# Block 1 of a four-block kernel: the queries and keys of the second sequence are projected in the four steps ahead of the first exponentials

## What is computed

```
qkv = (x @ Wqkv).reshape(Bx, Nx, 3, H, HD).transpose(2, 0, 3, 1, 4)
q, k, v = (qkv[0], qkv[1], qkv[2])
attn = jnp.einsum('bhnd,bhmd->bhnm', q, k) * (SCALE / TEMPERATURE)
attn = attn * alpha[None, :, None, None] + beta[None, :, None, None]
attn = jax.nn.softmax(attn, axis=-1) * gamma[None, :, None, None]
...
enhanced_v = v * (1.0 + ka)
out = jnp.einsum('bhnm,bhmd->bhnd', attn, enhanced_v)
```

## Time and profile before

| | |
|---|---|
| median of 3 runs | 2335.92 us (2332.85 to 2339.22) |
| the profiled execution | 2333.25 us, of which the span from first to last instruction is 2331.4 |
| PE busy | 2239.6 us, 96% of the span |
| DVE, ACT, POOL busy | 1635.1 (70%), 1254.6 (54%), 732.4 (31%) us |
| chain that ended last | PE 73%, DVE 14%, DMA 4%, ACT 4% |
| mean granted TensorE clock | 0.989 |

### The profile page before, as it was taken

The page is one execution under the profiler, slowest core; times in us unless marked ns, Lnnn a source line. Parts: engine busy times, 40 slices in busy tenths (PEclk is TensorE's granted clock), DMA queues, the critical chain, the costliest instruction groups (busy, mean ns, idle before and its releaser), DMA issues.

```text
span 2331.4 us, 42446 instructions
## 1 busy us (share of the span) xinstructions
PE 2239.6 (96%) x16257; PEld 1316.2 (56%) x16306; DVE 1635.1 (70%) x4252; ACT 1254.6 (54%) x2823; POOL 732.4 (31%) x730
## 2 busy tenths in 40 slices
PE   7999999999998999989899999999999999999998
PEld 3333333334634867756566666666666666666665
DVE  6788888886502746668777677677767777787763
ACT  4666666665222622247666656665665665566640
POOL 3344323321111411144433233333333333333321
PEclk7999999999998999999999999999999999999999
DMA  7454343333397020010000000000001000000001
GB/s 240 151 158 121 117 119 122 112 91 109 157 422 297 2 91 19 28 39 3 5 6 6 5 2 6 6 2 32 15 6 53 6 15 24 19 6 24 22 23 40
DMA packets 68617, 158.44 MB, mean 68 GB/s; under 512 B 6256, under 2 KB 49120, under 8 KB 63936
## 3 DMA queue, kind: packets, MB, share of 16 engines
q1 hardware_dynamic: 65856, 146.55, 17.8%
q0 software_dynamic: 2560, 9.18, 1.7%
HBM read 116.39 MB, written 35.13 MB: 65 GB/s over the span
## 4 chain that ended last, share of the span: by engine, by line
PE 73%; DVE 14%; DMA 4%; ACT 4%; issue 3%; POOL 1%; SPq 0%; another core or an unknown queue 0%; POOLq 0%; DVEq 0%; ACTq 0%
PE banks L2073 10%; PE banks L2051 7%; PE banks L1932 6%; PE banks L1946 5%; PE banks L232 4%; PE banks L274 4%; PE banks L2033 3%; PE banks L245 3%; PE banks L1976 3%; PE banks L1991 3%; DMA arena<-in_e_W 3%; DVE arena L483 2%; PE banks L1455 2%; PE banks L1958 2%; PE banks L300 2%
## 5 line engine op out<-in xcount | busy, mean ns | idle before, releaser
L483 DVE TENSOR_REDUCE arena<-banks 128x1 f32<-128x512 f32 x512 | 322.6, 681 | 61.2 <-PE banks L232 60.4
L395 ACT ACTIVATE arena<-banks 128x512 f32<-128x512 f32 x512 | 280.3, 596 | 136.1 <-PE banks L245 112.4
L2073 PE MATMUL banks<-arena 128*128 128x512 f32 x640 | 293.2, 594 | 1.0 <-DVE arena L2258 1.0
L2155 ACT ACTIVATE arena<-arena 128x256 f32<-128x256 f32 (+1 forms) x512 | 286.5, 562 | 5.0 <-DVE arena L2264 4.5
L2411 POOL TENSOR_TENSOR arena<-arena 128x512 f32<-128x512 f32 x128 | 162.8, 1272 | 379.8 <-DVE arena L2295 379.8
L1932 PE MATMUL banks<-arena 128*128 128x512 f32 x512 | 241.5, 594 | 2.8 <-DVE arena L2295 2.8
L232 PE MATMUL banks<-arena 96*128 96x512 bf16 x512 | 202.9, 400 | 14.6 <-DVE arena L483 8.9
L2407 POOL TENSOR_TENSOR arena<-arena 128x16 f32<-128x16 f32 x64 | 189.4, 2959 | 5.4
L2127 ACT ACTIVATE arena<-arena 128x256 f32<-128x256 f32 (+1 forms) x256 | 102.1, 471 | 162.9 <-DVE arena L2240 162.9
L2073 PEld LDWEIGHTS banks<-arena 128*128 128x128 f32 x640 | 115.5, 190 | 126.7 <-issue 116.5
L245 PE MATMUL banks<-arena 128*128 128x512 bf16 x463 | 174.6, 382 | 3.1 <-ACT arena L395 2.2
(11 more groups left out here) (304 smaller groups left out, 4225.7 us busy)
## 6 DMA issues: line engine op xcount, KB each, us to landing
arena<-in_e_W SPq DMA_DIRECT2D x16, 2048.0 KB, 15.6
arena<-stacks SPq DMA_DIRECT2D x64, 384.0 KB, 4.7
arena<-in_e_Wg SPq DMA_DIRECT2D x8, 2048.0 KB, 17.6
stacks<-arena SPq DMA_DIRECT2D x32, 384.0 KB, 2.5
stacks<-arena SPq DMA_DIRECT2D x32, 256.0 KB, 2.8
arena<-dens POOLq DMA_DIRECT2D x32, 256.0 KB, 4.8
arena<-in_xT SPq DMA_DIRECT2D x8, 512.0 KB, 7.8
stacks<-arena SPq DMA_DIRECT2D x32, 128.0 KB, 2.6
```

The lines of the kernel that those rows point to most:

```text
L395: e.activation(ex[:, j], self.psum[:, self.exp_bank1(k)], ACT.Exp).then_inc(s["a_e"], 1)
L483: e.tensor_reduce(split(self.maxima[n % 2][:, 0:16], TILES, UNIT)[:, t, j:j + 1], self.psum[:, k % 3], AX.X, ALU.max, negate=True).then_in ...
L2073: i = e.matmul(bank, weights[:, c], self.hT[:, c], start=c == 0, stop=c == 1)
L2155: k = e.activation(pr[:, h, at:], pr[:, h, at:], ACT.Exp, bias=mx[:, h:h + 1], scale=rn[:, h:h + 1], accum_out=den[:, h:h + 1])
```

## The change

The four tasks of halves 2 and 3 hang on steps (-1, 0), (-1, 1), (-1, 2) and (-1, 3), in the order 2 queries, 2 keys, 3 queries, 3 keys. Before, they hung on (0, 0), (0, 1), (2, 0) and (2, 1). Nothing else of the program text differs; the ring's order of banks follows from the table.

```diff
         if k + 1 < SEQS:
             for h in (0, 1):
                 for side in (0, 1):
-                    at[4 * k + 2 * h, side].append(("qk", 2 * k + 2 + h, side))
+                    at[(4 * k + 2 * h, side) if k else (-1, 2 * h + side)].append(("qk", 2 * k + 2 + h, side))
```

## The result

The changed kernel takes 2340.21 us (median of 20 runs, 2336.05 to 2349.72) where the kernel before takes 2334.76 (20 runs, 2329.35 to 2342.46). The ratio is 1.0021, with a 95% interval from 1.0011 to 1.0031: by it the change is slower by 4.9 us, between 2.6 and 7.2 (the two medians as they stand are 5.45 apart). The forecast was 1.2 us faster: the absolute time lies in the stated range, but the time moved the other way.

The account below looks back on a forecast made before the run. TensorE, busy for 96% of the span, was taken as the bound. +6.9 - 3.5 - 2.6 + 0.3 - 1.7 - 0.6 = -1.2 us, from the median 2335.92, gave 2334.7 us; range 2330 to 2341, the forecast's own 2332.5 to 2337.

Parts of the forecast that it names:

- term 1: End of the ramp: the first exponential comes 6.9 us later, 1.3 of it the exponential's table load.
- Terms 3 and 4: Step (0, 1): -2.6 us for the projection and bank wait removed, +0.3 us given back for the next step.
- Term 2: Step (0, 0): first exponential to first products with values takes 2.3 us instead of 5.8, -3.5 us.
- Terms 5 and 6: Unit 2: -1.7 us for the projection in (2, 0), -0.6 us for ScalarE's copy in (2, 1).
- term 5: Step (2, 0): one projection at full clock removed where the other engines wait for TensorE, -1.7 us.
- Term 6: Step (2, 1): ScalarE's copy of 0.58 us leaves its chain with the table loads, -0.6 us.
- The low clock through the ramp: Rival, steps (-1, 1) to (-1, 3): clock stays at half, about +5.3 us, 2341.2 us; chance 0.1.
- The late cuts: Rival: late cuts or stores make unit 1's exponentials wait 1 to 3 us, +0.8 us, 2336.7 us; chance 0.13.
- More is won: Rival: unit 2 gives all its TensorE time, exponentials start a microsecond earlier, about -4.6 us, 2331.3 us; chance 0.15.

Follow-up runs that it names:

- the experiment without half 3's products: Kernel before, with half 3's two projections at (2, 0) and (2, 1) each cut to one product of 16 columns: 2334.16 us, ratio 0.9996.
- half 2 alone: Changed kernel with only half 2's two tasks in the ramp, half 3's back at (2, 0) and (2, 1): 2335.62 us, ratio to before 1.0007.

## Why the prediction was wrong

**The bound and the ramp: right.** The projections fit where they were put, the clock rose early (two records of the keys of half 2 are 0.43 us apart), copies were not held by the cuts, and the order of events was the forecast one. The first exponential came 7.7 us later against the first maximum (57.44 - 49.31 - 0.43), for 6.9 in **term 1**: the clock rose at 45.7 us on the same scale and not at 44.3 to 44.7, so that three scores more went at half clock, and VectorE's maxima held each step's fourth score a little longer. The table load of 1.28 us was on the path, without the extra draining: the copy ends at 56.13, the load starts at 56.15, the exponential at 57.44. One reading was right with less ground than it seemed: in the earlier trace rows the prediction took the clock from distances of 0.86 and 0.43 us alone, while the profile's granted clock reads 1.00 in that stretch.

**The step that failed: that nothing happens to the clock behind a pause.** The prediction worked out TensorE's waits (56.2 us and the 1.88 us of the earlier trace rows, said to become longer) and then went on at full clock. That is where the sign turned: the half clock behind the two pauses costs 2.9 us in the first trace, and products that fill the pauses and shorten no wait take 2.9 us back in the trace and 4.8 in the median. By the traces this is firm for (2, 2), in five of five; behind (0, 0) the half clock came in two of five. It hid in the terms so (first traces of both kernels):
- **Terms 3 and 4**, together -2.3, measured -1.2: from the first products with values to the next 4.85 us (60.20 to 65.05) for 6.02 before. In it lie the 1.93 us of the first. **Term 2**, -3.5, measured -3.05 (57.44 to 60.20 is 2.76 for 5.81).
- **Terms 5 and 6**, together -2.3, measured +0.1; with the clock kept up, -1.3. Even at full clock 1.0 us is missing, nearly all of it in **term 5**, which credited the whole projection in (2, 0). TensorE takes 3.81 us from one group of products with values to the next (84.57 to 88.38) for 4.60 (80.67 to 85.27): 0.8 us, not 1.7. There VectorE is next: the maximum that TensorE waits for at 87.84 us stands behind VectorE's other work, and the pause is 0.58 us. **Term 6** held: with the products in the pause 0.5 us is won where 0.6 was forecast.

7.7 - 3.05 - 1.2 + 0.1 is 3.5 (rounded), the distance at the 97th maximum. From the forecast: -1.2 + 2.9 for the clock + 0.8 in term 1 + 1.0 in terms 5 and 6 is the same 3.5.

**The rivals.** The low clock through the ramp did not come. It named the right cause, the clock, at the wrong place; that its loss, 5.3 us, is near the measured 4.9 is luck, and so is it that the time lies in the stated range: that was widened for this rival, while the forecast's own ended at 2337. The late cuts did not matter: the second shift's load was issued at 66.22 for 64.1, and TensorE did not wait for it. "More is won" was wrong, and the experiment without half 3's products shows it most plainly.

**What stays open.** Of the 4.9 us, the traces place 3.0 (mean of all traces of either kernel) to 3.5 ahead of step (4, 0). Where the rest arises is not shown. The changed kernel had a late load or a further half clock in one or two later stretches in four of four traces, the kernel before in none of three; but a fourth trace of it has half clock at 137.1 us, and the variants have both, even those as fast as the kernel before. The products in the two pauses bring the median back by more than the trace explains (4.8 for 2.9 us). Neither what decides whether a pause of 1.5, 1.9 or 2.5 us draws half clock, nor why the load is late in some traces, is settled by these runs.

## What to carry to other kernels

Work put into a ramp comes ahead of what the ramp was to start: count the start of the steady state, and see which table load, copy or wait lay hidden ahead of it. Before work is taken out of a stretch, ask which engine is next there; if it is close, TensorE gets a pause and not time, and a pause can cost more than its own length. Work for nobody in such a pause tells the wait's price from the clock's; but take several traces of the unchanged kernel first, since a half clock that comes in two of five can be missing by chance.

## What the hardware showed unexpectedly

- Within or behind pauses of 1.5 and 3.8 us TensorE fell from 2.4 to 1.2 GHz, for 3.4 us or 6.8 us at a time: at the 3.8 us of (2, 2) in five of five traces, at the 1.5 us of (0, 0) in two of five. A pause of the same 1.88 us in (2, 2) did it in the kernel with half 2 alone and in none of four traces of the kernel before.
- With fifteen or eight unread products in the pause of (2, 2) the clock stayed at 1.00 there in all four traces that had them.
- Once (53.3 us, half 2 alone) the clock fell with no pause above 0.4 us, where scores went at VectorE's pace of 0.60 us; in both traces with four more products there it stayed up.
- The price of one such stretch of 3.4 us was 1.4 to 1.6 us (1.36 and 1.56 in the first trace).
